# Field sums of an attentional factorization machine: from four samples per full-array matmul to two samples in each of two row tiles

## What is computed

```
inner = x[:, row] * x[:, col]                     # 528 pairs of fields, each 128 values
fm = relu(inner @ attn_W.T + attn_b)              # per pair, 128 values
scores = sum(gnn * fm)                            # per pair
attn = softmax(scores over the 528 pairs)
pooled = 100 * sum over pairs of attn * inner     # per sample, 128 values
h = concat(gnn, pooled, gnn)
y = relu(relu(h @ W1 + b1) @ W2 + b2) @ W3
```

## Time and profile before

| | |
|---|---|
| time, median of 3 runs | 1273.08 us (1272.88 to 1273.84) |
| the profiled execution: its own time | 1276.58 us |
| its span, first to last instruction | 1274.3 us |
| granted TensorE clock, mean | 1.0 of full speed |
| busy: TensorE matmuls, VectorE, ScalarE, GpSimd | 95%, 90%, 80%, 37% |
| Fields matmuls with `attn_t`: records, busy | 480, 58.3 us |

### The profile page before, as it was taken

One profiled execution on the slowest core, in us unless ns is written; L12 is line 12 of the kernel. 1 busy time (PEld: TensorE's weight loads), 2 busy tenths in 40 slices (PEclk: granted clock), 3 DMA queues, 4 the chain that ended last, 5 costly groups with the idle time before them and its releaser, 6 DMA issues.

```text
span 1274.3 us, 21264 instructions
## 1 busy us (share of the span) xinstructions
PE 1207.8 (95%) x8752; PEld 902.5 (71%) x8752; DVE 1150.6 (90%) x643; ACT 1018.7 (80%) x1038; POOL 465.7 (37%) x271
## 2 busy tenths in 40 slices
PE   1499999999999999999999999999999999999998
PEld 1277777777777777777767777677776777777776
DVE  2399899998999989998999989999899998999974
ACT  1288998778887888878897788877888788887882
POOL 6586684018810387006840088102880000000000
PEclk9999999999999999999999999999999999999999
DMA  4213211311103111131102211031111300012100
GB/s 107 101 34 96 55 30 28 110 36 30 30 18 126 30 27 32 30 106 36 32 21 58 93 30 32 18 110 41 30 32 31 107 17 1 1 30 57 31 1 1
DMA packets 54287, 58.47 MB, mean 46 GB/s; under 512 B 10536, under 2 KB 48560, under 8 KB 53168
## 3 DMA queue, kind: packets, MB, share of 16 engines
q1 hardware_dynamic: 45728, 39.81, 10.5%
q0 software_dynamic: 8448, 17.32, 5.2%
q10 hardware_dynamic: 16, 0.00, 0.0%
HBM read 36.12 MB, written 17.31 MB: 42 GB/s over the span
## 4 chain that ended last, share of the span: by engine, by line
PE 78%; ACT 7%; issue 7%; DVE 6%; POOL 2%; DMA 0%; DVEq 0%; ACTq 0%; POOLq 0%
PE scores L564 18%; PE ring L534 16%; PE ring L541 12%; PE ring L542 11%; PE ring L543 11%; PE ring L592 3%; ACT fm L290 3%; DVE inner L405 3%; POOL x_rows L259 2%; PE ring L574 2%; ACT inner_hi L298 2%; DVE inner_lo L412 2%; PE ring L610 1%; DVE attn L447 1%; PE scores L621 1%
## 5 line engine op out<-in xcount | busy, mean ns | idle before, releaser
L290 ACT ACTIVATE fm<-ring,attn_b_sb 128x848 f32<-128x848 f32 (+1 forms) x640 | 596.9, 971 | 182.1 <-PE ring L534 175.7
L405 DVE TENSOR_TENSOR inner<-xt 128x2112 f32<-128x2112 f32 x256 | 602.7, 2354 | 67.5 <-ACT xt L328 37.4
L259 POOL DMA_INDIRECT x_rows<-in_tbl,ids_all x264 | 463.2, 1754 | 490.9 <-PE ring L574 401.2
L412 DVE TENSOR_TENSOR inner_lo<-inner,inner_hi 128x1688 fp32r<-128x1688 f32 (+4 forms) x256 | 467.0, 1824 | 25.8 <-ACT inner_hi L298 22.8
L541 PE MATMUL ring<-inner_hi,attn_wt_lo 128*128 128x424 f32 (+1 forms) x971 | 434.8, 448 | 4.2 <-ACT fm L290 3.5
L298 ACT CAST inner_hi<-inner 128x1688 fp32r<-128x1688 f32 (+4 forms) x256 | 392.3, 1532 | 5.1 <-DVE inner L405 5.0
L542 PE MATMUL ring<-inner_lo,attn_wt_hi 128*128 128x424 f32 (+1 forms) x971 | 344.3, 355 | 0.0
L543 PE MATMUL ring<-inner_hi,attn_wt_hi 128*128 128x424 f32 (+1 forms) x971 | 344.1, 354 | 0.0
L534 PE MATMUL ring<-inner,attn_wt 128*128 128x424 f32 (+1 forms) x618 | 276.6, 544 | 10.2 <-issue 6.5
L564 PE MATMUL scores<-fm,gnn_blocks 128*32 128x264 f32 x4096 | 254.6, 389 | 5.5 <-ACT exp_pairs L305 5.5
L541 PEld LDWEIGHTS ring<-inner_hi,attn_wt_lo 128*128 128x128 f32 x971 | 182.8, 188 | 71.8 <-issue 39.1
(11 more groups left out here) (50 smaller groups left out, 250.3 us busy)
## 6 DMA issues: line engine op xcount, KB each, us to landing
x_dram<-x_rows SPq DMA_DIRECT2D x8, 2112.0 KB, 6.6
x_fields<-x_dram SPq DMA_DIRECT2D x120, 128.0 KB, 3.0
x_rows<-in_tbl,ids_all POOLq DMA_INDIRECT x264
attn_t<-attn_turned SPq DMA_DIRECT2D x112, 32.0 KB, 1.9
w_sb<-in_W_top SPq DMA_DIRECT2D x2, 512.0 KB
x_rows<-x_dram SPq DMA_DIRECT2D x8, 128.0 KB, 3.9
x_fields<-in_r_gnn_feature SPq DMA_DIRECT2D x1, 512.0 KB
h<-in_W_top SPq DMA_DIRECT2D x1, 256.0 KB
```

Source lines behind the costliest of these rows:

```text
L259: nc.gpsimd.indirect_dma_start(out=x_rows[:, f, :], out_offset=None, in_=tables[f], in_offset=bass.IndirectOffsetOnAxis(ap=ids_all[:, t, f ...
L290: nc.scalar.activation(dst, slot(("hidden", pair, j))[:, :, 0:n], ACT.Relu, bias=attn_b_sb[:, 0:1]).then_inc(s_fm, 1)
L405: nc.vector.tensor_tensor(dst, a, b, ALU.mult).then_inc(s_inner, 1)
L412: nc.vector.tensor_tensor(inner_lo[:, S % LO_BUFS, 0:COLS - at], inner[:, S % INNER_BUFS, at:], inner_hi[:, S % HI_BUFS, 0:COLS - at].bitc ...
```

## The change

Each of a job's 8 matmuls over 128 partitions is replaced by two over 64 partitions (`for h in range(2)`): half h contracts over the partitions of samples 2h and 2h+1, has the field rows of these as 64 x 128 weights, streams 64 columns (2 samples x 32) and writes PSUM bank h of the slot. `attn_t` and `attn_t_tail` halve in size: sample q uses column block q % 2. To have the outputs lie by sample, the order of samples changes: row group q of a job now holds 8 successive samples, and a step takes every eighth sample of a quarter tile (`first`, and the stride FN in `product`) in place of four successive ones. `load_fields` reads 8 successive rows per row group in place of every fourth. `gnn_block` follows the new order with four copies of 4 x 8 columns in place of two of 4 x 16.

```
-        attn_t = sb("attn_t", [P, 2, QS, FN, I])
+        attn_t = sb("attn_t", [P, 2, 2, FN, I])
...
-                    first = t * P + QS * FN * c + q
-                    rows = x_dram[first:first + QS * (FN - 1) + 1:QS, 1:F, :]
+                    first = t * P + QS * FN * c + FN * q
+                    rows = x_dram[first:first + FN, 1:F, :]
...
-                    sp.dma_start(attn_t[own, c % 2, q], attn_turned[own, c * FN:(c + 1) * FN, :])\
+                    sp.dma_start(attn_t[own, c % 2, q % 2], attn_turned[own, c * FN:(c + 1) * FN, :])\
...
-                x = xt[:, t % 2, GROUPS * s:GROUPS * (s + 1), :]
+                first = QS * FN * (s // FN) + s % FN
+                x = xt[:, t % 2, first:first + FN * (GROUPS - 1) + 1:FN, :]
...
-                g = gnn_t[:, t * P:(t + 1) * P].rearrange("a (s j) -> a j s", j=GROUPS)
+                g = gnn_t[:, t * P:(t + 1) * P].rearrange("a (c j n) -> a c j n", j=GROUPS, n=FN)
...
-                nc.vector.tensor_scalar(low, g[:, :, 0:STEPS // 2], 1.0, None, ALU.mult)
...
+                for c in range(FJ // 2):
+                    nc.vector.tensor_scalar(low[:, :, c * FN:(c + 1) * FN], g[:, c], 1.0, None, ALU.mult)
+                for c in range(FJ // 2):
+                    last = g[:, FJ - 1 - c, :, FN - 1:FN]
+                    src = bass.AP(tensor=g.tensor, offset=last.offset, ap=[last.ap[0], last.ap[1], [-1, FN]])
+                    done = nc.vector.tensor_scalar(high[:, :, c * FN:(c + 1) * FN], src, 1.0, None, ALU.mult)
+                done.then_inc(s_blocks, 1)
...
-                    h, to = divmod(n * QS * I, 512)
-                    last = nc.tensor.matmul(bank[:, h, to:to + QS * I], x[:, n, :], own[:, :, n, :], start=True, stop=True)
+                    for h in range(2):
+                        rows = slice(h * 2 * I, (h + 1) * 2 * I)
+                        dst = bank[:, h, :].rearrange("d (r n i) -> d r n i", r=2, n=FN)[:, :, n, :]
+                        last = nc.tensor.matmul(dst, x[rows, n, :], own[rows, :, n, :], start=True, stop=True)
```

More of the change, by code:

```diff
@@ L122, in afm_tower @@
         TAIL_INNER = (ALL - 3) % INNER_BUFS
-        attn_t_tail = inner[:, TAIL_INNER, 0:2 * QS * FN * I].rearrange("p (c q n i) -> p c q n i", c=2, q=QS, n=FN)
+        attn_t_tail = inner[:, TAIL_INNER, 0:2 * 2 * FN * I].rearrange("p (c q n i) -> p c q n i", c=2, q=2, n=FN)
         x_fields_tail = x_rows[:, 0:2 * FN, :].rearrange("p (c n) d -> p c n d", c=2)
@@ L381, in _ @@
                 own = slice(q * I, (q + 1) * I)
-                nc.scalar.copy(attn_t[own, :, q], attn_turned[own, 0:2 * FN, :].rearrange("p (c n) i -> p c n i", c=2))\
+                nc.scalar.copy(attn_t[own, :, q % 2], attn_turned[own, 0:2 * FN, :].rearrange("p (c n) i -> p c n i", c=2))\
                     .then_inc(s_tail_attn, 1)
@@ L385, in _ @@
                 own = slice(q * I, (q + 1) * I)
-                nc.scalar.copy(attn_t_tail[own, :, q], attn_turned[own, 2 * FN:, :].rearrange("p (c n) i -> p c n i", c=2))\
+                nc.scalar.copy(attn_t_tail[own, :, q % 2], attn_turned[own, 2 * FN:, :].rearrange("p (c n) i -> p c n i", c=2))\
                     .then_inc(s_tail_attn, 1)
@@ L415, in gnn_block @@
             def gnn_block(t):
-                g = gnn_t[:, t * P:(t + 1) * P].rearrange("a (s j) -> a j s", j=GROUPS)
+                g = gnn_t[:, t * P:(t + 1) * P].rearrange("a (c j n) -> a c j n", j=GROUPS, n=FN)
                 low = gnn_blocks[:, :, 0:34 * (STEPS // 2 - 1) + 1:34]
                 high = gnn_blocks[:, :, 32:32 + 33 * (STEPS // 2 - 1) + 1:33]
-                nc.vector.tensor_scalar(low, g[:, :, 0:STEPS // 2], 1.0, None, ALU.mult)
-                src = bass.AP(tensor=g.tensor, offset=g[:, :, STEPS - 1:STEPS].offset,
-                              ap=[g.ap[0], g.ap[1], [-g.ap[2][0], STEPS // 2]])
-                nc.vector.tensor_scalar(high, src, 1.0, None, ALU.mult).then_inc(s_blocks, 1)
+                for c in range(FJ // 2):
[5 more added lines that the diff above has]
+                done.then_inc(s_blocks, 1)
             def row_max(t):
@@ L507, in _ @@
                 own = slice(q * I, (q + 1) * I)
-                nc.vector.tensor_copy(attn_t[own, :, q], attn_turned[own, 0:2 * FN, :].rearrange("p (c n) i -> p c n i", c=2))\
+                nc.vector.tensor_copy(attn_t[own, :, q % 2], attn_turned[own, 0:2 * FN, :].rearrange("p (c n) i -> p c n i", c=2))\
                     .then_inc(s_tail_attn, 1)
@@ L511, in _ @@
                 own = slice(q * I, (q + 1) * I)
-                nc.vector.tensor_copy(attn_t_tail[own, :, q], attn_turned[own, 2 * FN:, :].rearrange("p (c n) i -> p c n i", c=2))\
+                nc.vector.tensor_copy(attn_t_tail[own, :, q % 2], attn_turned[own, 2 * FN:, :].rearrange("p (c n) i -> p c n i", c=2))\
                     .then_inc(s_tail_attn, 1)
```

## The result

The changed kernel takes 1280.92 us in the median of ten executions (1275.72 to 1282.25), against 1273.08 before: 1.0047 times as long, with a 95% interval of 1.0031 to 1.0063. It is slower, by about 6 us by the ratio. The ten times stand in two groups, and this is the first thing to explain: four lie at 1275.7 to 1276.4 with a mean granted clock of 0.999 to 1.000, six at 1280.9 to 1282.3 with 0.995. The profiled execution is one of the short ones (1275.88 us, span 1273.9).

A forecast was written before the change was run, and what follows sets the result against it. The prediction took TensorE (95% busy) as the bound, with VectorE near; 7 tiles x (0.36 us Fields jobs + 0.11 us copies) = 3.3 us on the median of 1273.08 gave 1276.4 us, +0.26%, range 1261 to 1284.

The forecast's parts named there:

- The loads pace the record: Fields matmuls on TensorE: loading 128 weight columns takes 0.11 us, as much as a record, so halved streaming saves nothing.
- the body: A Fields job's loads and matmuls: row tiles load side by side, 1.76 us against 1.78 before, so no change.
- a change into row tiles and back: Around a Fields job on TensorE: entry costs 0.20 us, exit at odd steps 0.15 us.
- the 0.09 us of standstill: TensorE's halt when tiling mode changes, read from hidden stage to reduction: 0.28 us to the first load against 0.19.
- What reaches the end: Pipeline jobs per tile: 0.15 us from each even-step job (10, 16), 0.06 and 0 from odd ones (7, 13); 0.36 in all.
- `gnn_block`: VectorE's copies at the start of a tile: four in place of two, counted in full as +0.11 us per tile.
- The sum of 3.3 us: Whole kernel: 7 tiles x (0.36 from Fields jobs + 0.11 from the copies).
- GpSimd's zeroing in the tail: Zeroing in the tail, taken as halved by the change and ending long before what waits for it: nothing.
- The tail: Four last Fields jobs: no switch shows, and jobs of 1.8 us hide under VectorE's 2.58 us pace: nothing.
- Free switches: Rival, Fields jobs: loads overlap and switches are free or hidden; 0 to -1.4 us, 1272 to 1273.5 us; chance 0.22.
- serial loads: Rival, Fields jobs: loads of the two row tiles go one after another; +55 us, 1328 us; chance 0.15.
- the halved body: Rival, Fields jobs: a 64-row load takes half the time, a job 0.89 us; -11 us, 1262 us; chance 0.10.

The follow-up runs named there:

- half_pipe: The changed kernel with full-array Fields matmuls everywhere, those of the 28 pipeline jobs streaming 64 of 128 columns: 1275.67 us, ratio 0.9993 to the kernel before.
- mix_alt: The changed kernel with full-array tail jobs and each pipeline job's 8 matmuls alternating between full array and row tiles: 1307.08 us, ratio 1.0235 to the kernel before.
- v_pipe: The changed kernel with row tiles in the 28 pipeline jobs alone and full-array matmuls in the tail: 1275.58 us, ratio 1.0019 to the kernel before.
- v_full: The changed kernel without row tiles: full-array Fields matmuls everywhere, new sample order, loads and four copies kept: 1273.79 us, ratio 1.0006 to the kernel before.
- hmajor_pipe: Row tiles in the pipeline alone, each job issuing all 8 matmuls of row tile 0 before those of row tile 1: 1334.71 us, ratio 1.0451.
- half_tail: The changed kernel with full-array Fields matmuls everywhere, the tail's four jobs streaming 64 of 128 columns: 1276.69 us, ratio 1.0014 to the kernel before.
- keep_between: The changed kernel with a pair of waiting matmuls behind each row-tiled tail job and one fewer behind them all: 1284.18 us, ratio 1.0063 to the kernel before.
- odd_only: The changed kernel with row tiles only in the 14 pipeline jobs at odd steps (7 and 13), full-array matmuls elsewhere: 1273.61 us, ratio 1.0002 to the kernel before.
- after: The changed kernel's first measurement and profile: median 1280.92 us, ratio 1.0047 to the kernel before; the profiled execution took 1275.88 us.
- again: The changed kernel run once more with no edit: median 1276.16 us of nine, ratio 1.0047 to the kernel before.
- mix_blocks: The changed kernel with full-array tail jobs and each pipeline job issuing 4 full-array matmuls, then 4 in row tiles: 1278.85 us, ratio 1.0016 to the kernel before.
- v_tail: The changed kernel with row tiles in the tail's four Fields jobs alone, full-array matmuls in the pipeline: 1278.63 us, ratio 1.0037 to the kernel before.

## Why the prediction was right, and what it left out

**The pipeline: right in mechanism and size.** The loads pace the record (half_pipe); the two row tiles load side by side (the load row above), and the body didn't change; a change into row tiles and back costs 0.34 us (mix_alt) where 0.35 was forecast, and the start of a job 0.28 us behind the last hidden matmul fits the 0.09 us of standstill in it. The Trainium skill's rule that a change of tiling mode drains TensorE (TensorEngine Tiling (Array Packing), Key Properties) holds for row tiles by those rows. The same page's factor of up to two for 64 or fewer (Theoretical Speedup) does not show: neither two row tiles nor half the streamed columns shortened a job of float32 matmuls with 128 weight columns by more than 0.06 us.

**What reaches the end: right.** I had 0.36 us per tile, 0.30 from even and 0.06 from odd jobs; measured are 0.31 by v_pipe against v_full, 0.27 from even and 0.04 from odd, the last of them within the scatter.

**`gnn_block`: the term was mis-sized in what reaches the end.** The copies take 0.09 us more on VectorE, 0.11 forecast, but the period grows by about 0.04 at most; VectorE's 0.16 us of idle time has shrunk to 0.07 and covered it. The sum of 3.3 us is 2.4 by measurement of v_pipe against the kernel before.

**A detail was misread.** I wrote that GpSimd's zeroing in the tail halves. The change leaves it as it is, and it takes 1807 ns after it, 1811 before. Nothing waits for it.

**The tail: "Nothing" was wrong.** The step looked at the switches and at VectorE's distance of 2.58 us and didn't ask what the tail's jobs do to the clock. In 10 of the 19 executions of the changed kernel they cost about 5.5 us more: 1281 to 1282 in place of 1276. The prediction's point of 1276.4 us is where the short group lies, and the measured ratio, 1.0047 in place of 1.0026, is the mean over both. That the range held is owed to its width, not to a case in it: no rival had a clock in it.

**Free switches, serial loads and the halved body** did not happen: a job starts 0.28 us behind the last hidden matmul and not 0.19, and takes 1.93 us and not 3.5 or 0.9. hmajor_pipe shows that serial loads would have come as soon as the row tiles had not taken turns.

**Open.** Why one execution falls into the long group and the next doesn't was not settled. With 64 streamed columns in the tail, a mean clock of 0.993 to 0.995 came in 10 of 19 executions of the changed kernel, 8 of 12 with row tiles in the tail alone, 2 of 6 of half_tail and 3 of 6 of keep_between; with 128 in the tail in none of 45 executions of v_full, v_pipe, odd_only and half_pipe. The record holds a clue. The short dip ahead of the tail's jobs, seen above in the changed kernel, is not peculiar to it: hmajor_pipe aside, the mean clock is 0.999 in each kept profile that has it (after, again, keep_between, mix_blocks, mix_alt) and 1.000 in each that has no low stretch, and mix_blocks, with 128 columns in its tail, has it too (0.50 from 1250 to 1252 us). By their mean clocks 17 of the 45 executions with 128 columns have the dip and 28 nothing; of the 43 with 64 columns 18 have it, 23 are long and only 2 have nothing. So the long ones seem to be those that had no dip just before, which nothing here tested. Also open is how the 58 us of hmajor_pipe divide. No version here that computes the whole result beats the kernel before: v_full and odd_only can't be told from it.

## What to carry to other kernels

Before halving what a matmul streams, read what paces it: if two weight loads with nothing between them start as far apart as the records of the stream, fewer streamed columns buy nothing, and every change of tiling on a busy TensorE costs a standstill and an unhidden load each way. Price each switch by what stands behind it, since half of them here were free. And where a kernel holds its clock by hand in a tail, treat each shape in that tail as part of the clock, and read times execution by execution: a median between two groups tells of neither.

## What the runs showed of the hardware that was not expected

TensorE's clock fell to its lower level while the trace has TensorE busy without a break: in v_tail at 0.54 and 0.50 in stretches with 3.00 of 3.00 us busy and loads running all the time. Before it fell TensorE had streamed 64 columns per load in place of 128, in row tiles here; half_tail, without row tiles, has executions with the same mean clock of 0.995. The Trainium skill has the clock follow how busy TensorE has recently been (TensorE: Matmul & The Clock Gate, Part 1); by these rows, being busy in the profile's sense is not the measure.

Loads of the two row tiles overlap only when their matmuls alternate: 32 records took 1.93 us in turns and 3.32 us one tile after the other.
